# Two packed 32-bit words for each edge, sorted by minimum and maximum alone, in a graph network on one core

## What is computed

```python
edge_index = stack([src, dst])                    # row = src, col = dst
h = maximum(layernorm(x), 0.0)
for t in range(2):
    m_input  = concatenate([h[col], h[row], edge_attr], axis=1)
    messages = m_input @ msg_W[t].T + msg_b[t]
    agg      = segment_sum(messages, row, num_segments=12500)
    h        = gru_cell(agg, h, gru_Wih[t], gru_bih[t], gru_Whh[t], gru_bhh[t])
out = x + h
```

## Time and profile before

| | us |
|---|---|
| median of three runs | 2558.26 (2556.83 to 2558.97) |
| the profiled execution | 2556.8 |
| its span, first to last instruction | 2555.1 |
| VectorE busy | 2312.2 (90%) |
| ScalarE busy | 2103.5 (82%) |
| TensorE busy | 1619.5 (63%) |
| GpSimd busy | 608.0 (24%) |

### The profile page before, as it was taken

One profiled execution on the slowest core, in us unless ns is written; L12 is line 12 of the kernel. 1 busy time (PEld: TensorE's weight loads), 2 busy tenths in 40 slices (PEclk: granted clock), 3 DMA queues, 4 the chain that ended last, 5 costly groups with the idle time before them and its releaser, 6 DMA issues. The chain is left out here.

```text
span 2555.1 us, 126468 instructions
## 1 busy us (share of the span) xinstructions
PE 1619.5 (63%) x47260; PEld 1526.9 (60%) x47260; DVE 2312.2 (90%) x3824; ACT 2103.5 (82%) x4269; POOL 608.0 (24%) x853
## 2 busy tenths in 40 slices
PE   0000000000002399999999999977899999999996
PEld 0000000000001398999999999967899999999996
DVE  5999999999993699999999999977899999999995
ACT  6657787666653599999999999977899999999996
POOL 0000000000005343445445454430111111111111
PEclk9999999999999699999999999998999999999998
DMA  7000000210004366666666677646677677677773
GB/s 137 0 0 0 0 0 13 63 23 20 0 0 121 100 231 223 227 228 224 232 226 228 224 227 231 229 140 222 205 237 237 238 238 238 238 237 238 238 238 118
DMA packets 175417, 400.69 MB, mean 157 GB/s; under 512 B 73071, under 2 KB 76789, under 8 KB 174855
## 3 DMA queue, kind: packets, MB, share of 16 engines
q1 hardware_dynamic: 116907, 204.17, 25.4%
q0 software_dynamic: 57296, 195.19, 22.9%
q10 hardware_dynamic: 1132, 0.27, 0.1%
HBM read 384.63 MB, written 14.57 MB: 156 GB/s over the span
## 5 line engine op out<-in xcount | busy, mean ns | idle before, releaser
L1102 ACT ACTIVATE rows<-ps_rows 128x512 f16<-128x512 f32 x2744 | 1453.1, 638 | 64.0 <-PE ps_rows L1025 41.0
L1042 PE MATMUL ps_sum<-rows,src 128*64 128x132 f16 (+1 forms) x21952 | 1151.5, 225 | 15.7 <-ACT rows L1102 9.8
L1042 PEld LDWEIGHTS ps_sum<-rows,src 128*64 128x64 f16 x21952 | 901.9, 142 | 27.5 <-ACT rows L1102 18.4
L1195 DVE TENSOR_TENSOR src<-iota_units,src_lane 128x2048 f16<-128x2048 f16 (+1 forms) x784 | 862.4, 1100 | 43.6 <-PE ps_sum L1042 43.4
L1025 PE MATMUL ps_rows<-rows_next,dst 128*64 128x128 f16 x10976 | 548.8, 220 | 40.2 <-DVE dst L1186 22.3
L1025 PE MATMUL ps_rows<-rows_now,dst 128*64 128x128 f16 x10976 | 542.6, 219 | 18.1 <-DVE dst L1186 10.3
L775 PE MATMUL ps_src<-ident,late 112*64 112x112 f32 x98 | 29.2, 332 | 803.9 <-DVE late L837 803.0
L1186 DVE TENSOR_SCALAR dst<-lanes,lane_no 128x2048 f16<-128x2048 f16 (+1 forms) x784 | 532.2, 679 | 4.9 <-DMA lanes<-lanes_dram 3.9
L775 PEld LDWEIGHTS ps_src<-ident,late 112*64 112x64 f32 x98 | 14.3, 146 | 806.5 <-DVE late L837 803.9
L1025 PEld LDWEIGHTS ps_rows<-rows_next,dst 128*64 128x64 f16 x10976 | 413.9, 111 | 63.3 <-issue 29.7
L1025 PEld LDWEIGHTS ps_rows<-rows_now,dst 128*64 128x64 f16 x10976 | 408.3, 111 | 41.2 <-issue 13.3
(11 more groups left out here) (180 smaller groups left out, 2236.3 us busy)
## 6 DMA issues: line engine op xcount, KB each, us to landing
lanes<-lanes_dram POOLq DMA_DIRECT2D x294, 512.0 KB, 4.8
lanes<-lanes_dram SPq DMA_DIRECT2D x294, 512.0 KB, 4.7
lanes<-lanes_dram POOLq DMA_DIRECT2D x98, 256.0 KB, 4.1
lanes<-lanes_dram SPq DMA_DIRECT2D x98, 256.0 KB, 4.1
rows_now<-parts_dram SPq DMA_DIRECT2D x112, 32.0 KB, 1.7
rows_next<-parts_dram SPq DMA_DIRECT2D x112, 32.0 KB, 3.7
parts_dram<-rows_now SPq DMA_DIRECT2D x1, 3136.0 KB, 16.2
sorted_dram<-planes SPq DMA_DIRECT2D x1, 3136.0 KB, 11.7
```

Of the source, the lines that this page charges most:

```text
L1042: last = nc.tensor.matmul(ps_sum[b][at, 0:width], hot[:, at], row, start=(j == 0), stop=(j == J - 1))
L1102: nc.scalar.activation(rows[:, (u + NU * b) % ring, 0:n, 0:2 * H], cut(ps_rows[(u + NU * b) % 4][:])[:, 0:n, :], ACT.Copy).then_inc(rows_r ...
L1195: nc.vector.tensor_tensor(src1[q][:, 0:len(units)], iota_units[:].rearrange("p (o l) k -> p o l k", o=1) .broadcast_to([P, len(units), P, ...
```

## The change

Edge planes become words of 32 bits. A place (13 bits and the float's sign, offset so that all are normal numbers, the lower half of the nodes counted down with the sign set, the upper half counted up) stands in the upper bits of both words. Word a carries below it the lane (7 bits) and the lower 11 bits of the weight as a fixed-point number; word b carries the weight's upper bits. Both words are read as float32, and each passes the network by itself: within one source the two orders may differ, which leaves the sum of weights of a source as it was.

In block one, after the sources have landed (VectorE), and after the weights:

```diff
+                dve.wait_ge(src_in, 48)
+                nc.vector.tensor_scalar(word_a, src_i[:], -1.0, float(TH - 1 + OFF), ALU.mult, ALU.add)...
+                step(nc.vector.tensor_scalar(scratch, src_i[:], float(TH), -2.0 ** 31, ALU.is_lt, ALU.mult))
+                nc.vector.scalar_tensor_tensor(out=word_b, in0=src_i[:], scalar=float(OFF - TH), in1=word_a, ...)
+                nc.vector.scalar_tensor_tensor(out=placed, in0=word_b, scalar=31 - TOP, in1=scratch, ...)
...
+                step(nc.vector.tensor_reduce(units[:, 0:1], attr_in, AX.X, ALU.max, apply_absolute_value=True))
...
+                step(nc.vector.tensor_scalar(scratch, attr_in, units[:, 2:3], 2.0 ** 27, ALU.mult, ALU.mult))
+                step(nc.vector.tensor_scalar(word_b, scratch, 3, TOP + 1, ALU.logical_shift_left, ALU.logical_shift_right))
+                nc.vector.tensor_tensor(word_b, word_b, placed, ALU.bitwise_or).then_inc(words_ready, 1)
+                nc.vector.scalar_tensor_tensor(out=word_a, in0=scratch, scalar=0x7FF, in1=placed, ...)
```

The weights are loaded ahead of `dst`, each with its own semaphore. ScalarE's copy of the weights at the start of block two (line 546) goes. A step of the sort, first ScalarE, then VectorE:

```diff
-                    nc.scalar.activation(packed(held[n % 2], blocks, run), low_val, ACT.Copy).then_inc(held_ready, 1)
+                    act.wait_ge(lows_ready[0], n + 1)
+                    act.wait_ge(highs_ready[0], n + 1)
+                    nc.scalar.activation(low_a, packed(lows[0][n % 2], blocks, run), ACT.Copy).then_inc(lows_back[0], 1)
+                    act.wait_ge(lows_ready[1], n + 1)
+                    act.wait_ge(highs_ready[1], n + 1)
+                    nc.scalar.activation(low_b, packed(lows[1][n % 2], blocks, run), ACT.Copy).then_inc(lows_back[1], 1)
                     if n in WIDE:
                         first_job(WIDE.index(n))
-                    act.wait_ge(highs_ready, n + 1)
-                    nc.scalar.activation(low, packed(lows[n % 2], blocks, run), ACT.Copy).then_inc(lows_back, 1)
-                    if n in WIDE:
                         second_job(WIDE.index(n))
...
-                    nc.vector.tensor_tensor(swap, low, high, ALU.is_gt).then_inc(compared, 1)
-                    wait(dve, lows_back, n - 1)
-                    nc.vector.tensor_tensor(packed(lows[n % 2], blocks, run), low, high, ALU.min).then_inc(lows_ready, 1)
...
-                    nc.vector.tensor_tensor(high, low, high, ALU.max).then_inc(highs_ready, 1)
-                    dve.wait_ge(held_ready, n + 1)
-                    nc.vector.copy_predicated(low_val, swap, high_val).then_inc(first_swap, 1)
-                    dve.wait_ge(first_swap, n + 1)
-                    nc.vector.copy_predicated(high_val, swap, packed(held[n % 2], blocks, run)).then_inc(swapped, 1)
+                    wait(dve, lows_back[0], max(before, n - 1))
+                    wait(dve, highs_ready[0], before)
+                    nc.vector.tensor_tensor(packed(lows[0][n % 2], blocks, run), low_a, high_a, ALU.min)...
+                    wait(dve, lows_back[1], max(before, n - 1))
+                    wait(dve, highs_ready[1], before)
+                    nc.vector.tensor_tensor(packed(lows[1][n % 2], blocks, run), low_b, high_b, ALU.min)...
+                    dve.wait_ge(lows_ready[0], n + 1)
+                    nc.vector.tensor_tensor(high_a, low_a, high_a, ALU.max).then_inc(highs_ready[0], 1)
+                    dve.wait_ge(lows_ready[1], n + 1)
+                    nc.vector.tensor_tensor(high_b, low_b, high_b, ALU.max).then_inc(highs_ready[1], 1)
```

In the spread a group unpacks a word, and the weights are turned by a true matmul with a diagonal of each partition's unit in place of a transpose:

```diff
-                        last = nc.tensor.transpose(ps_attr[...], slots_of[0:C, s // 2, s % 2, :, 1], ident[0:C, 0:C])
+                        last = nc.tensor.matmul(ps_attr[...], slots_of[0:C, s // 2, s % 2, :, 1], unit_ident[0:C, 0:C], ...)
...
-                    step(nc.vector.tensor_tensor(apart[g % 2]..., slots_of[0:C, pair_at, :, :, 0], tile_base..., ALU.subtract))
-                    step(nc.vector.tensor_copy(whole, apart[g % 2][0:C, 0:n, :]))
-                    step(nc.vector.tensor_scalar(dst_part[0:C, 0:n, :], whole, P - 1, None, ALU.bitwise_and))
-                    nc.vector.tensor_scalar(whole, whole, 7, None, ALU.arith_shift_right).then_inc(dst_ready, 1)
-                    nc.vector.tensor_copy(apart[g % 2][0:C, 0:n, :], whole).then_inc(src_ready, 1)
+                    nc.vector.tensor_scalar(in_pairs_of(dst_part), word, 11, P - 1, ALU.logical_shift_right, ALU.bitwise_and)...
+                    step(nc.vector.tensor_scalar(place, word, 31 - TOP, None, ALU.arith_shift_right))
...
+                        step(nc.vector.tensor_tensor(src_part[:, split_at:], place[:, split_at:], own_bases..., ALU.subtract))
+                    step(nc.vector.tensor_scalar(attr_bits, attr_bits, TOP + 1, TOP + 1, ALU.logical_shift_left, ALU.arith_shift_right))
+                    step(nc.vector.tensor_scalar(word, word, 0x7FF, None, ALU.bitwise_and))
+                    nc.vector.scalar_tensor_tensor(out=slots_of[0:C, pair_at, :, :, 1], in0=attr_bits, scalar=2048.0, in1=word, ...)
```

More of the change, by code:

```diff
@@ L35 @@
 LO = 2048.0
+ATTR_TOP = 16.0
+NOWHERE = 1.75 * 2.0 ** 127
 UJ = 4
@@ L263, in build @@
         dst_i = sb("dst_i", [P, SORTED], I32, scope=sort_scope)
-        lane_f, attr_in = late[:, 0, 0:EW], late[:, 1, 0:EW]
+        lane_i, attr_in = late[:, 0, 0:EW].bitcast(I32), late[:, 1, 0:EW]
+        word_a, word_b = [planes[:, v, 0:EW].bitcast(I32) for v in range(2)]
+        scratch = attr_room[:, 0:EW].bitcast(I32)
+        placed = late[:, 0, 0:EW].bitcast(I32)
         src_in = sem("src_in")
@@ L616, in second_job @@
                         normed(some(job - ROOT - 1, 0, 8, 8))
-                for n, before, blocks, run, (low, high, low_val, high_val) in steps():
-                    act.wait_ge(vals_ready, 2)
-                    wait(act, swapped, before)
+                for n, before, blocks, run, (low_a, high_a, low_b, high_b) in steps():
+                    act.wait_ge(pads_ready, 2)
                     if n == FIRST_STEPS:
@@ L655, in _ @@
                 nc.vector.tensor_scalar(spans[:], spans[:], 8, None, ALU.arith_shift_right).then_inc(first_known, 1)
-                dve.wait_ge(keys_ready, 2)
-                dve.wait_ge(vals_ready, 2)
-                for n, before, blocks, run, (low, high, low_val, high_val) in steps():
-                    swap = packed(wrong[n % 2], blocks, run)
+                dve.wait_ge(words_ready, 3)
+                dve.wait_ge(pads_ready, 2)
+                for n, before, blocks, run, (low_a, high_a, low_b, high_b) in steps():
                     if n == WIDE[SQUARES]:
@@ L678, in _ @@
                         nc.vector.tensor_tensor(rest, h[:, :, 0:H], parts[:, :, 0:H], ALU.subtract).then_inc(norms_ready, 1)
-                    wait(dve, lows_back, before)
-                    wait(dve, swapped, before)
                     if n == FIRST_STEPS:
@@ L775, in _ @@
                         nc.tensor.transpose(ps_src[k % 2][0:SLOTS, i * C:(i + 1) * C], apart[g % 2][0:C, s - GROUPS[g][0], :], ident[0:C, 0:C])
-                        last = nc.tensor.transpose(ps_attr[k % 2][0:SLOTS, i * C:(i + 1) * C], slots_of[0:C, s // 2, s % 2, :, 1], ident[0:C, 0:C])
+                        last = nc.tensor.matmul(ps_attr[k % 2][0:SLOTS, i * C:(i + 1) * C], slots_of[0:C, s // 2, s % 2, :, 1], unit_ident[0:C, 0:C],
+                                                start=True, stop=True)
                     last.then_inc(slots_ps, 1)
@@ L836, in _ @@
-                    dve.wait_ge(dst_ready, g + 1)
-                    nc.vector.tensor_copy(apart[g % 2][0:C, 0:n, :], whole).then_inc(src_ready, 1)
+                    nc.vector.tensor_scalar(in_pairs_of(dst_part), word, 11, P - 1, ALU.logical_shift_right, ALU.bitwise_and).then_inc(dst_ready, 1)
+                    place = in_pairs_of(apart[g % 2].bitcast(I32))
+                    step(nc.vector.tensor_scalar(place, word, 31 - TOP, None, ALU.arith_shift_right))
+                    split_at = min(max(MID // 2 - group[0] // 2, 0), n // 2)
```

117 lines of the change are left out of this document (76 added, 41 removed).

## The result

| | median of runs, us | lowest to highest | profiled execution | its span |
|---|---|---|---|---|
| before | 2558.61 (4 runs) | 2556.83 to 2559.35 | 2556.8 | 2555.1 |
| after | 2526.52 (4 runs) | 2517.32 to 2528.77 | 2528.8 | 2527.2 |

The ratio is 0.9864, 95% interval 0.9848 to 0.9881. The change makes the kernel faster, by 32 us (1.4%), where 78 were forecast (2480, range 2460 to 2506): right in sign, wrong in size, and outside the range. The same four stages, read as windows of the changed kernel. Their ends are the first step's first instruction, the last maximum, the first unpacking of gathered words, and the last of ScalarE's copies in the spread; the third and fourth row together answer to the third of the earlier trace rows.

The account below looks back on a forecast made before the run. The sort was taken as a chain on VectorE (busy 696.3 of 718.9 us). From 2556.8 us: block one and two +12, sort -106, spread +18, rounds unchanged, giving 2480.8, stated as 2480, range 2460 to 2506.

Parts of the forecast that it names:

- That is +0.3 each, 1.2 for four tiles: Spread, TensorE: the weights' transposes become true float32 matmuls, each 0.3 us dearer, 1.2 us for four tiles.
- Two packs of four tiles: Spread: the dearer matmuls show in only two packs of each group, +2.2 us; ends one pack (1.2), all six (7.2).
- Ends: ... +45: Spread: forecast +18 us over four groups, with a cheap end of +8 and a dear end of +45.
- The rival of dear ends (2514): Block one and spread at their dear ends, +19 and +45 us instead of 12 and 18: 2514 us; chance 0.14.
- The sort: Sort window 612.7 us against 718.9, 106 less: VectorE's 520.9 and 9.5 plus waits for ScalarE by order of jobs.
- Jobs hidden: Rival: in the sort ScalarE hides its jobs by load, not order; sort 537 us, time 2405; chance 0.04.
- the waits show: Rival: in the sort VectorE loses 0.10 us at each instruction; sort 58 us longer, time 2538; chance, wholly or half, 0.10.
- Block one: Start, before the sort: making the words on VectorE adds 12 us; +11 with single operations at 2.0, +19 at the dear end.
- The chain in the spread: VectorE's operations in each group before TensorE may start: +3 us taken, between +1.7 and +4.9.
- The rounds: Last stage: code and data unchanged, only edge order within a source differs, so 1675.7 us as before.
- The sign that was set for them: If the rounds are longer than 1676 us, the forecast was wrong in kind.

Follow-up runs that it names:

- e2: The changed kernel with the sources also turned by true matmul, so TensorE never alternates kinds; 2520.6 us (1 run).
- e10: The changed kernel with weights transposed again, VectorE's first unpacking waiting until the gathers of all four groups have landed; 2507.0 us (1 run).
- e5: The changed kernel with all 49 of ScalarE's counting passes before the sort; 2657.5 us (1 run), sort 579.2 us.
- e7: The changed kernel with weights transposed again, 8 counting passes before the sort, none before the regrouping, normalised rows one wide step later; 2465.3 us, ratio 0.9545.
- e11: The changed kernel with each pack as two transposes, two true matmuls, two transposes, two true matmuls; 2536.4 us (1 run).
- e4: The changed kernel with weights transposed again, the factor applied by one more VectorE operation per group; 2493.6 us (ratio 0.9663), again 2483.5 us (0.9617).

## Why the prediction was wrong

- *The step that failed* is the spread's "That is +0.3 each, 1.2 for four tiles. It shows only while TensorE is what the copies wait for; I take two packs of four tiles in each group, +2.2". The mechanism was named and its size was wrong, in three ways. The true matmul of 112 columns has 0.37 of its own, 0.19 more than a transpose, so 0.3 was rather dear. (The 0.49 behind it was scaled from a duration, start to end, while the 0.19 of a transpose is from start to start; in e2 a true matmul lasts 0.58 and the next one starts after 0.375.) But each turn between the kinds adds 0.33 a tile, which no term held; so it was +0.52 a tile against the slow pace of before. And TensorE stayed at that pace, so that against the faster packs it was +0.70. I had the alternation before me in the diff, one transpose and one true matmul a tile, and priced the two as if each stood among its own kind. The Trainium skill says, in Perfetto Trace Analysis, "Transposes", to do a logical transpose by transpose and not by a standard matmul. The runs agree, at 52 us: the changed kernel's stretch is 140.6 and that of e10, with transposes alone and no late signal, 88.3. I had not weighed it.
- *"Two packs of four tiles"* failed with it: at 3.57 us a pack against 0.80 of copies, TensorE is what VectorE waits for in all six packs of all four groups. The copies that were to hide it are shorter than even my own dear price for a pack (4 x 0.68 = 2.7 us). That could have been seen: 2.7 is above 0.80 for every pack, and the end "all six" was the plain reading of my own numbers. (Two packs at 1.2 are also 2.4 and not 2.2, 0.8 us over the four groups.)
- *"Ends: ... +45"* was built from the same price, six packs at 1.2, so the range could not reach +64. In time the result lies between the rivals of 2514 and 2538. The second, waits that show in the sort, did not come at all. The rival of dear ends (2514) was the nearest in kind, in one of its two parts: TensorE's pace, but not the strided operands, and not block one, which came at its cheap end.
- *The sort* was right in sum, 610.3 for 612.7, and in its terms: neighbours overlap by 0.08, the three long waits were 7.1, 6.6 and 8.0, e5 and e7 moved it as the rules of order say. The smaller waits were 6 us less than summed and VectorE's own time 3 more, which took part of each other away. *Jobs hidden* (537) and *the waits show* (671) fell.
- *Block one*: +9.6, near the +11 given for single operations at 2.0. The text ahead of the prediction and the prediction speak of seven full-width instructions; they are eight, four with one tensor and four with two, and the sum did count eight.
- *The chain in the spread*: +1.7 and not the +3 taken, but +3.7 in the fourth group.
- *The rounds* were to cost what they did and took 7.0 us more. Over the thirteen profiles they are 1670 to 1684 us: 1670 to 1674 in the four with transposed weights in the new layout, 1677 and 1681 in those of before, 1680 to 1684 with true matmuls. By instructions they are the same. What makes them differ wasn't tried. The sign that was set for them (longer than 1676 means wrong in kind) was too tight: the kernel before stands at 1677 and 1681 by the same cut.

Against the sum of 2480.8 the start is 2.4 us cheaper, the sort 2.6, the spread 46.1 dearer and the rounds 7.0: 48.1, the whole miss. With e10's stretch of 88.3 in place of 140.6, that is with transposes alone and no late signal, the changed kernel would have come to an estimated 2476, near the forecast.

## What to carry to other kernels

When a change swaps the kind of one of two operations that alternate on an engine, price the pair as it will stand in the list, not each from rows where it stood among its own kind: here the neighbour that was not touched went from 0.19 to 0.33 us. If both kinds are needed, group them; going from four turns a pack to one gave 1.0 us of 3.57, and doing without the second kind gave more. And compare a term's own period (2.7 us a pack) with the cover that is to hide it (0.80) before deciding for how many repeats it shows.

## What the runs showed of the hardware that was not expected

- A true matmul of float32 (two entries) and a transpose that follow each other in turn cost 0.56 + 0.33 us for 112 columns; among their own kind 0.37 and 0.19. The weight loads show an idle of 0.20 and 0.28 before each, where nothing recorded was waited for; in e11 it is 0.33 and 0.28 at each change of kind, and within the packs of e2, all of one kind, there is none.
- The granted clock did not always tell the pace. In the changed kernel's spread the column reads 1.00 throughout (2.4 GHz) while each transpose takes 0.33. The second run of e4 read 1.00 too in its first packs, where starts were 0.19 apart up to 714.3 and 0.095 from there on. In its last group starts were 0.19 apart up to 796.1 and 0.095 from there on; two windows there, the clock in the column behind GpSimd's:

```profile
792.00:797.00 5.00, 5.00 (x31) 4.80 (x32) 1.92 (x6) 1.80 (x6) 0.00 (x0) 0.57 0.00 0
797.00:802.00 5.00, 2.72 (x25) 1.98 (x22) 3.21 (x9) 4.17 (x10) 0.00 (x0) 1.00 0.00 0
```

  Here it went from 0.50 (1.2 GHz) to 1.00 with the pace, while transposes ran one behind the other; in the first group it did not show the slow pace. (0.57 is the mean over a window with the change in it; in the kernel before, from 817 to 826 us and with starts 0.19 apart, it is 0.50.) So the column follows the pace once it has risen for the first time, and reads 1.00 at either pace until then. In the changed kernel it never falls in the spread, so it can't say which level the slow pace there was.
- TensorE's signal to ScalarE and VectorE could come 3 to 25 us after the last recorded matmul while GpSimd's 49 gathers were running or just over, 16 to 39 us in all (each wait counted whole). That was so in ten profiles; the two first ones, of before and after, had none with packs and gathers side by side as well. In e10, where no pack ran beside a gather, there was none.
- Single-tensor int32 operations of VectorE that read or write every second word kept 0.96 us for 1,536 elements; every fourth word took 3.40 for 3,584. With 1,664 elements those that work in place took 1.09, and those that read every second word and write into another tensor 1.88, in ten profiles of ten.
